# LSTM input products of two steps as seven block products in place of eight, and the LSTM one tick further behind the RNN

## The reference

```python
h_t = tanh(h_prev @ Wh + x_t @ Wx + b)            # RNN, h_0 = cond
y = x + h                                          # for all steps
a = y_t @ WxL + bL + h_prev @ WhL                  # LSTM, 4 x 512 columns
i, f, o = sigmoid(a[:, 0:512]), sigmoid(a[:, 512:1024]), sigmoid(a[:, 1024:1536])
g = tanh(a[:, 1536:])
c = f * c_prev + i * g
h = o * tanh(c)                                    # h = cond, c = 0 at the start
out = y + h
```

## Time and profile before

| | |
|---|---|
| time, median of 3 runs | 885.91 us (884.77 to 885.98) |
| the profiled execution's own time | 885.89 us |
| its span in the profile | 884.1 us |
| busy: TensorE, VectorE | 864.2 us (98%), 742.1 us (84%) |
| busy: ScalarE, GpSimd | 395.6 us (45%), 225.2 us (25%) |

### The profile page before, as it was taken

How to read it: one execution, slowest core, us unless ns; L and a number is a source line. 1 busy time by engine, 2 the same in 40 slices (tenths; PEclk the granted TensorE clock), 3 DMA queues, 4 the chain that set the end, 5 groups by cost and what they waited for, 6 DMA issues and landing times.

```text
span 884.1 us, 42307 instructions
## 1 busy us (share of the span) xinstructions
PE 864.2 (98%) x18608; PEld 511.6 (58%) x18608; DVE 742.1 (84%) x1965; ACT 395.6 (45%) x1062; POOL 225.2 (25%) x503
## 2 busy tenths in 40 slices
...
GB/s 317 260 3 26 27 14 15 27 27 27 27 19 17 20 27 27 26 27 15 15 27 27 27 27 15 18 24 26 27 28 27 15 3 15 15 16 15 15 14 13
DMA packets 38649, 30.06 MB, mean 34 GB/s; under 512 B 4268, under 2 KB 37184, under 8 KB 37184
## 3 DMA queue, kind: packets, MB, share of 16 engines
...
q10 hardware_dynamic: 160, 0.08, 0.0%
...
## 4 chain that ended last, share of the span: by engine, by line
PE 89%; DVE 6%; issue 2%; ACT 1%; DMA 0%; ACTq 0%; POOL 0%; POOLq 0%; DVEq 0%
PE ps_l L790 35%; PE ps_l L818 33%; PE ps_r L859 8%; PE ps_r L876 8%; PE ps_l L807 1%; PE ps_r L842 1%; PE ps_r L832 1%; DVE pre_l L623 1%; ACT gates L430 1%; PE ps_l L904 1%; DVE h_hi L645 0%; ACT tanh_c L437 0%; DVE fc L630 0%; DVE ig L632 0%; DVE c L634 0%
## 5 line engine op out<-in xcount | busy, mean ns | idle before, releaser
L818 PE MATMUL ps_l<-wxl_hi,whl_raw 128*32 128x512 f16 x3840 | 251.3, 379 | 0.0
L818 PEld LDWEIGHTS ps_l<-wxl_hi,whl_raw 128*32 128x32 f16 x3840 | 104.0, 97 | 101.9
L317 POOL TENSOR_TENSOR xb<-xb,h_l 128x128 f32<-128x128 f32 x128 | 59.1, 461 | 324.5 <-DVE h_l L651 324.5
L790 PE MATMUL ps_l<-whl_hi,hT_hi 128*32 128x512 f16 x2016 | 132.3, 379 | 3.9 <-DVE hT_hi L649 3.1
L790 PE MATMUL ps_l<-whl_lo,hT_hi 128*32 128x512 f16 x2016 | 132.2, 379 | 0.0
L790 PE MATMUL ps_l<-whl_hi,hT_lo 128*32 128x512 f16 x2016 | 132.2, 379 | 0.0
L344 POOL TENSOR_TENSOR yT<-xT,hT_r 128x128 f32<-128x128 f32 x124 | 58.7, 474 | 270.1 <-DVE hT_r L691 270.1
L623 DVE SCALAR_TENSOR_TENSOR pre_l<-ps_l,g_products,bias_l 128x256 f32<-128x256 f32 x240 | 105.0, 479 | 25.1 <-PE ps_l L790 18.5
L818 PE MATMUL ps_l<-wxl_lo,whl_raw 128*32 128x512 f16 x1920 | 125.7, 379 | 0.0
L442 ACT ACTIVATE h_r<-pre_r 128x128 f32<-128x128 f32 x128 | 39.5, 309 | 152.3 <-DVE pre_r L674 118.0
L674 DVE SCALAR_TENSOR_TENSOR pre_r<-ps_r,g_products,xr 64x128 f32<-64x128 f32 x224 | 76.3, 341 | 18.5 <-POOL xr L330 16.8
...
## 6 DMA issues: line engine op xcount, KB each, us to landing
xb<-in_x SPq DMA_DIRECT2D x128, 64.0 KB, 2.0
out<-xb SPq DMA_DIRECT2D x128, 64.0 KB, 1.8
...
pre_r<-in_L_cond_b ACTq DMA_DIRECT2D x1, 2.0 KB
```

The lines of the kernel that those rows point to most:

```text
L317: nc.gpsimd.tensor_tensor(xb[g % NX][:, t, :], xb[g % NX][:, t, :], h_l[s % 2][:, :], ALU.add).then_inc(out_done, 1)
L790: last = nc.tensor.matmul(ps_l[s % 2][quarter(j), :], (hT_hi, hT_lo)[h_part][:, k, :], gate_slice(whl[w_part][k], j), start=False, stop=(h ...
L818: last = nc.tensor.matmul(ps_l[s % 2][quarter(j), :], y16[y_part][g % 2][:, k, t * B:(t + 1) * B], gate_slice(wxl[w_part][k], j), start=(y ...
```

## The change

From LSTM step S2 = 24 on, two steps s and s + 1 are treated as a pair. The chunks of the width are taken as two halves, the weight's columns as two halves (gates i, f and gates o, g), and the two steps as two rows of blocks. The 2 x 2 by 2 x 2 product of blocks, eight products, becomes seven by a form of Strassen's algorithm. Each of the seven has 6 combinations of parts and chunks by 4 quarters, with 256 columns.

- *Weights.* Four differences of weight blocks (T1 to T4) are formed in place on GpSimd (`t_piece`, 32 of 256 columns, ticks 15 to 25), and split on ScalarE (`t_block_high`, 8 of 1024 columns) and VectorE (`t_block_low`, 8 of 1024 columns), ticks 18 to 27.
- *Inputs.* `add_yT` writes the turned y in blocks, and `y_in_blocks` forms four sums of blocks on GpSimd, 128 columns each, at the end of every fourth tick from 27. `y_hi` and `y_lo` split seven blocks (896 columns) in place of 512.
- *Products.* `pair_first`, `pair_second`, `pair_third` and `pair_last` are spread over ticks s + 5, s + 6, s + 6 and s + 7. Their sums are made in PSUM, now with four banks: a bank is zeroed or given the bias beforehand, and a partial sum is copied from one half of a bank to the other (`zero_first`, `bias_second`, `copy_m1`, `copy_m7`), or taken out (`take_u2`, `take_u4`), six ScalarE operations of 256 columns a pair. `add_in_21` on GpSimd (256 columns) completes what the second step adds in place of the bias.
- *Order.* From tick 31 TensorE does `product_r16(k + 1)` ahead of `recurrent_r16(k)`.
- *Lag.* LAG goes from 7 to 8, and the tables of the first ticks shift a little; the scale of the LSTM's weights has two bits more headroom.
- *`add_out`* waits for `h_lo` as well.

The core of the diff:

```diff
-LAG = 7
+LAG = 8
...
+S2 = 24
...
-        ps_l = [bank("ps_l0"), bank("ps_l1")]
+        def t_halves(home):
+            return [home[:, part * H * 2:(part + 1) * H * 2].bitcast(F16).rearrange("p (k n) -> p k n", k=2) for part in (0, 1)]
+        tw = {n: t_halves(home) for n, home in zip((1, 2, 3, 4), (whl_raw[0], whl_raw[1], whl_raw[2], wr_raw[OF_X]))}
+        yA = [wr_raw[OF_H][:, i * 8 * P:(i + 1) * 8 * P].rearrange("p (a k q b) -> p a k q b", a=8, k=2, q=2) for i in range(2)]
+        yS = [[wxl_raw[0][:, (2 * part + i) * 448:(2 * part + i + 1) * 448].bitcast(F16) for i in range(2)] for part in (0, 1)]
+        HALF = 2 * P
+        zeros, bias_diff, u2 = [wxl_raw[1][:, i * HALF:(i + 1) * HALF] for i in range(3)]
+        in_21 = [wxl_raw[1][:, (3 + i) * HALF:(4 + i) * HALF] for i in range(2)]
+        in_22 = [wxl_raw[1][:, (5 + i) * HALF:(6 + i) * HALF] for i in range(2)]
+        ps_l = [bank(f"ps_l{i}") for i in range(4)]
...
+        T_ORDER = (1, 3, 2, 4)
+        T_MADE_AT = {15 + i: range(3 * i, min(3 * i + 3, 32)) for i in range(11)}
+        T_HIGH_AT = {18: [(1, 0)], 19: [(1, 1)], 20: [(3, 0)], 21: [(3, 1)], 23: [(2, 0)], 24: [(2, 1)], 26: [(4, 0), (4, 1)]}
+        T_LOW_AT = {19: [(1, 0)], 20: [(1, 1)], 21: [(3, 0)], 22: [(3, 1)], 24: [(2, 0)], 25: [(2, 1)], 26: [(4, 0)], 27: [(4, 1)]}
+        CONST_AT = 27
...
+        def pair_at(k):
+            s = k - LAG + 3
+            return (s - S2) // 2 if S2 <= s < T and s % 2 == 0 else None
+        IN_PAIRS = S2 + LAG - 1
+        def pair_step(p):
+            return S2 + 2 * p
...
                 pool.wait_ge(lstm_h, s + 1)
+                if N0 <= s + 1 < T:
+                    pool.wait_ge(lstm_lo, s + 2 - N0)
                 nc.gpsimd.tensor_tensor(xb[g % NX][:, t, :], xb[g % NX][:, t, :], h_l[s % 2][:, :], ALU.add).then_inc(out_done, 1)
...
+            def t_piece(i):
+                n, chunk, cols = T_ORDER[i // 8], i % 8 // 4, i % 4 * HALF
+                if i == 0:
+                    pool.wait_ge(xl_mm, S1 - 1)
+                    pool.wait_ge(w_split[OF_X], J)
+                if i % 8 == 0:
+                    wait(pool, t_made, i)
+                top, bottom = wxl_raw[chunk], wxl_raw[2 + chunk]
+                left, right = slice(cols, cols + HALF), slice(GH // 2 + cols, GH // 2 + cols + HALF)
+                dst, a, b = {1: (top[:, left], top[:, right], top[:, left]),
+                             3: (top[:, right], bottom[:, right], top[:, right]),
+                             2: (bottom[:, right], bottom[:, right], top[:, left]),
+                             4: (bottom[:, left], bottom[:, left], bottom[:, right])}[n]
+                nc.gpsimd.tensor_tensor(dst, a, b, ALU.subtract).then_inc(t_made, 1)
...
+            def y_block(g, out, a, b, op):
+                y = yA[g % 2]
+                nc.gpsimd.tensor_tensor(y[:, out, :, :, :], y[:, a, :, :, :], y[:, b, :, :, :], op).then_inc(y_blocks, 1)
+            def y_in_blocks(g):
+                done = 4 * (g - G2)
+                pool.wait_ge(yT_done, TG * (g + 1))
+                y_block(g, 4, 0, 1, ALU.add)
+                y_block(g, 6, 2, 0, ALU.subtract)
+                pool.wait_ge(y_blocks, done + 1)
+                y_block(g, 5, 4, 2, ALU.subtract)
+                pool.wait_ge(y_blocks, done + 3)
+                y_block(g, 7, 3, 5, ALU.subtract)
+            def add_in_21(p):
+                pool.wait_ge(const_done, 2)
+                pool.wait_ge(u2_out, p + 1)
+                pool.wait_ge(lstm_pre, 2 * (pair_step(p) - 2))
+                nc.gpsimd.tensor_tensor(in_21[p % 2], u2, bias_diff, ALU.add).then_inc(in_21_done, 1)
...
+                for i in T_MADE_AT.get(k, []):
+                    t_piece(i)
+                if k == CONST_AT:
+                    constants()
+                if pair_at(k - 1) is not None:
+                    add_in_21(pair_at(k - 1))
                 if k < T:
                     add_yT(k)
                     add_y(k)
+                    if k % TG == TG - 1 and k // TG >= G2:
+                        y_in_blocks(k // TG)
...
+                nc.scalar.activation(tw[n][0][:, chunk, :], t_block(n, chunk), ACT.Copy,
+                                     scale=w_scale[:, OF_X:OF_X + 1]).then_inc(t_high, 1)
...
+            def zero_first(p):
+                s = pair_step(p)
+                act.wait_ge(const_done, 2)
+                act.wait_ge(lstm_pre, 2 * (s - 3))
+                nc.scalar.activation(ps_l[s % 4][:, 0:HALF], zeros, ACT.Copy).then_inc(a_zeroed, 1)
+            def bias_second(p):
+                s = pair_step(p)
+                act.wait_ge(lstm_pre, 2 * (s - 2))
+                g, _ = group(s)
+                nc.scalar.activation(ps_l[(s + 1) % 4][:, HALF:GU], bias_l[:, HALF:GU], ACT.Copy,
+                                     scale=g_inverses[:, 0, g:g + 1]).then_inc(b_biased, 1)
+            def copy_m1(p):
+                bank_a = ps_l[pair_step(p) % 4]
+                act.wait_ge(m1_mm, p + 1)
+                nc.scalar.activation(bank_a[:, HALF:GU], bank_a[:, 0:HALF], ACT.Copy).then_inc(m1_copied, 1)
+            def copy_m7(p):
+                bank_b = ps_l[(pair_step(p) + 1) % 4]
+                act.wait_ge(m7_mm, p + 1)
+                nc.scalar.activation(bank_b[:, 0:HALF], bank_b[:, HALF:GU], ACT.Copy).then_inc(m7_copied, 1)
+            def take_u2(p):
+                s = pair_step(p)
+                g, _ = group(s)
+                act.wait_ge(m6_mm, p + 1)
+                wait(act, in_21_done, p)
+                nc.scalar.activation(u2, ps_l[s % 4][:, HALF:GU], ACT.Copy, scale=unscale[:, g:g + 1]).then_inc(u2_out, 1)
+            def take_u4(p):
+                s = pair_step(p)
+                g, _ = group(s)
+                act.wait_ge(m5_mm, p + 1)
+                act.wait_ge(lstm_pre, 2 * (s - 2))
+                nc.scalar.activation(in_22[p % 2], ps_l[s % 4][:, HALF:GU], ACT.Copy, scale=unscale[:, g:g + 1]).then_inc(u4_out, 1)
...
+                    if pair_at(k) is not None:
+                        zero_first(pair_at(k))
+                    if pair_at(k - 1) is not None:
+                        take_u2(pair_at(k - 1))
                     cell_tanh(k - LAG)
+                    for n_t, chunk in T_HIGH_AT.get(k, []):
+                        t_block_high(n_t, chunk)
...
+                    copy_m1(pair_at(k))
+                    bias_second(pair_at(k))
+                if pair_at(k - 1) is not None:
+                    copy_m7(pair_at(k - 1))
+                    take_u4(pair_at(k - 1))
...
+                    nc.vector.scalar_tensor_tensor(out=yS[1][g % 2], in0=yA[g % 2][:, 1:8, :, :, :].rearrange("p a k q b -> p (a k q b)"),
+                                                   scalar=g_scale[:, OF_X, g:g + 1], in1=yS[0][g % 2],
+                                                   op0=ALU.mult, op1=ALU.subtract).then_inc(y_split, 1)
...
+            def t_block_low(n, chunk):
+                dve.wait_ge(t_high, 2 * T_ORDER.index(n) + chunk + 1)
+                nc.vector.scalar_tensor_tensor(out=tw[n][1][:, chunk, :], in0=t_block(n, chunk), scalar=w_scale[:, OF_X:OF_X + 1],
+                                               in1=tw[n][0][:, chunk, :], op0=ALU.mult, op1=ALU.subtract).then_inc(t_split, 1)
...
+                added = [bias_l[:, 0:HALF], bias_l[:, HALF:GU]]
+                if s >= S2 and s % 2:
+                    p = (s - S2) // 2
+                    added = [in_21[p % 2], in_22[p % 2]]
+                    dve.wait_ge(in_21_done, p + 1)
+                    dve.wait_ge(u4_out, p + 1)
...
+            def block_product(p, n, parts, done=None):
+                s = pair_step(p)
+                g, t = group(s)
+                block = {1: 1, 2: 2, 3: 6, 4: 0, 5: 3, 6: 4, 7: 5}[n]
+                at, half = {1: (s, 0), 2: (s, 0), 3: (s, 1), 5: (s, 1), 6: (s, 1), 4: (s + 1, 0), 7: (s + 1, 1)}[n]
+                for y_part, w_part, k in parts:
+                    stationary = yS[y_part][g % 2].rearrange("p (a k q b) -> p a k q b", a=7, k=2, q=2)[:, block, k, t // 2, :]
+                    if n == 1:
+                        weights = wxl[w_part][k][:, 0:GH // 2]
+                    elif n == 2:
+                        weights = wxl[w_part][2 + k][:, 0:GH // 2]
+                    elif n == 3:
+                        weights = wxl[w_part][2 + k][:, GH // 2:GH]
+                    else:
+                        weights = tw[{4: 4, 5: 1, 6: 2, 7: 3}[n]][w_part][:, k, :]
+                    weights = weights.rearrange("p (g j u) -> p j g u", g=2, j=J)
+                    for j in range(J):
+                        last = nc.tensor.matmul(ps_l[at % 4][quarter(j), half * HALF:(half + 1) * HALF], stationary,
+                                                weights[:, j, :, :], start=False, stop=(y_part == 1 and k == 1),
+                                                skip_group_check=True)
+                if done is not None:
```

(41 more changed lines are left out.)

88 lines of the change are left out of this document (72 added, 16 removed).

## The result

The changed kernel takes 912.54 us (median of 4 runs, 912.00 to 913.93) against 885.94 us before, measured beside it: a ratio of 1.0301, with a 95% interval of 1.0281 to 1.0322. It is 26.6 us slower. The forecast was 903.5, with a range of 867 to 914.

The account below looks back on a forecast made before the run. TensorE bounds the kernel before, and a nearly as long VectorE/GpSimd ring was to bound the changed one: span 884.1 + 1.6 (lag) + 7 (T blocks) + 9 (steady part) = 901.7, plus 1.8 around it, 903.5 us; range 867 to 914.

Parts of the forecast that it names:

- TensorE's saving: Input products of two steps: 4.62 us in place of 5.18, removing 0.28 us a tick, 29 us over 52 pairs.
- rival D: TensorE's seven products cost as much as eight, smaller pieces waiting on ScalarE's copies; given no chance of its own.
- The VectorE/GpSimd ring: Steady ticks: VectorE's program order, with pre_r behind GpSimd's add_out and bias add; 6.03 us a plain tick, 26.4 a four.
- C+4.50: Forecast start of pre_r in a plain tick, in us after that tick's pre_l starts.
- The collision: Every fourth tick: GpSimd's block sums delay VectorE's fc, ig, c and hT_r_lo, making h_hi 0.9 us later.
- B (nothing): Block sums cost VectorE nothing: ring 25.5 us per four, 880.5 us in all; chance 0.20 with its partial form.
- C (1.8): Each block sum stops VectorE for all its 0.46 us: ring 27.3 per four, 925 us; chance 0.07, or worse.
- The T blocks: Ticks 15 to 27: subtractions and low parts delay GpSimd's bias add; +7 us, between 3 and 12.
- The lag: One tick more of lag: RNN-only tick +4, one LSTM tick less at the start -8.3, tail +5.8; +1.6 us.
- a sign of being wrong: Start of the kernel: a first pre_l more than 5 us later than 38.54 would show the forecast wrong.
- My 9: Steady part, ticks 29 to 127: 24.75 fours at 26.4 in place of 26.06 us, given as +9 us.
- A (TensorE the bound): Steady ticks: TensorE stays the bound, faster, with four ticks of 24.9 us; 865.5 us in all; chance 0.23.

Follow-up runs that it names:

- e2: The changed kernel with add_bias_r16 ahead of add_out in GpSimd's order: 904.59 us, ratio to before 1.0189.
- e3: The changed kernel with block sums of 4 columns in place of 128, other columns left unsummed: 896.75 us, ratio to before 1.0100.
- e1: The changed kernel without add_out's new wait for h_lo: 920.01 us, ratio to before 1.0359.
- e8: e2, and in every fourth tick copy_m7 and take_u4 behind rnn_tanh in ScalarE's order: 896.58 us, ratio to before 1.0116.
- e6: The changed kernel with the T blocks' eight low parts cut from 1024 to 32 columns, products reading high parts instead: 905.57 us, ratio to before 1.0215.
- e7: The changed kernel with the 32 subtractions making the T blocks cut from 256 to 8 columns each: 910.38 us, ratio to before 1.0271.
- e4: The kernel before with LAG = 8 and the changed kernel's weight tables, nothing else: 892.34 us, ratio to before 1.0050.
- e5: The changed kernel with e2 and e3 together: 887.74 us, ratio to before 1.0016.

## Why the prediction was right, and where it was off

- **TensorE's saving** came as worked out: 27.3 ns a matmul of 256 columns, and 6.22 and 6.19 us in the ticks that TensorE sets (e2). That answers rival D: a pair's 168 matmuls take 4.58 us, as forecast.
- **The VectorE/GpSimd ring** is longer than that, as forecast. In the plain tick from 407.65, `pre_r` starts at 412.21, C+4.56 (forecast C+4.50), and the tick takes 6.10 (forecast 6.03). Four ticks: forecast 26.4, measured 26.26. `turn_x` and `x16_lo` ticks were forecast at 6.4, and took 6.31 and 6.42, and ticks 29 to 127 average 6.61 (forecast 6.6).
- **The collision** of the block sums with `fc`, `ig`, `c` and `hT_r_lo` is shown by e3: 0.6 us a time, which answers rivals B (nothing) and C (1.8). Forecast 0.9; `h_hi` was 0.63 late, as `fc` to `hT_r_lo` stood still by 0.14 to 0.27 each, not 0.31. The Trainium skill's rule (SBUF — State Buffer, "SBUF: two separate sides") has whole instructions excluding each other. The trace agrees that the two hold each other up, and e3 that this is what costs, but not that VectorE stands still for all of the 0.46 us of a GpSimd addition.
- **`y_hi` costed at nothing** was right in size only by luck: I said that its work hides behind `pre_r`, and it ends in the same moment as `pre_r`, within 0.01 us. The path through ScalarE is as long as the one I worked out. e1, e2 and e8 show that this queue counts once `pre_r` comes sooner.
- **The T blocks**: +7 forecast. Low parts and subtractions measured 7.0 and 2.5 (e6, e7), and of the rest of the +12.6 I hadn't counted tick 30: with a whole input product and two pieces of the first pair, it is 2.1 us over.
- **The lag**: here a step failed. I priced the start as "one LSTM tick less, 8.3, and one RNN tick more, 4". In the changed kernel the RNN tick more cost 5.3 (the first `pre_l` comes 5.28 later, which is past the 5 us that I had named as a sign of being wrong) and the LSTM tick less gave back 5.3, all of it by tick 10, so the start got no shorter. e4 gives 5.8 for the lag in all by its medians, 3.1 to 5.8 by its interval, and 5.3 between the two profiles. What holds ticks 8 and 9 I only read from the trace (the low parts of the recurrent weights); no run tried it. That term was 1.6 and should have been between 5 and 6.
- **The last tick**, 1.4 us longer by TensorE's clock, was in no term.

Together: the steady part gave 6.7 where I had 9, the T blocks and tick 30 12.6 where I had 7, the lag and the tail 7.75 where I had 1.6. My 9 was itself rounded up: 24.75 x (26.4 - 26.06) is 8.4. So the forecast was 9 us too low, with an error of 2.3 one way and two of about 6 the other; the measured time is only 1.5 us inside the upper end of the range. Of the rivals, A (TensorE the bound) needs both causes gone: e5, with 887.7 us, still has one tick of 6.6, the T blocks and the lag.

**Where the gain went.** TensorE does give back 0.28 us a tick. VectorE, GpSimd and ScalarE take it back in the steady part with 0.36 (four ticks of 26.26 over 24.8), and the fixed price of some 20 us (T blocks, tick 30, lag, tail) comes on top.

What stays open: why e1 loses 1.4 us in ticks 16 to 32, and what it is that holds ticks 8 and 9 of the start.
